# Turning the inverse softmax sums of the two larger tiles with a 32x32 block transpose, so that the context's factor is read in order

## The reference, cut to what matters

```python
scores = einsum('blhe,bmhe->bhlm', Q, K) / sqrt(E)
attn = softmax(scores + mask)                       # exp(..) / sum over the keys
ctx = einsum('bhlm,bmhe->blhe', attn, V)            # one context vector per token and head
y = gelu(ctx @ Wo + bo)
```

## Time and profile before

| | us |
|---|---|
| median of 3 runs | 646.54 (646.0 to 646.78) |
| the profiled execution, its own time | 644.08 |
| its span from the first to the last instruction | 642.3 |
| TensorE busy in the span | 604.5 (94%) |
| VectorE / ScalarE / GpSimd busy | 476.5 (74%) / 428.2 (67%) / 304.3 (47%) |
| share of the 16 DMA engines' time on queue q1 | 63.2% |

### The profile page before, as it was taken

One profiled execution on the slowest core, in us unless ns is written; L12 is line 12 of the kernel. 1 busy time (PEld: TensorE's weight loads), 2 busy tenths in 40 slices (PEclk: granted clock), 3 DMA queues, 4 the chain that ended last, 5 costly groups with the idle time before them and its releaser, 6 DMA issues.

```text
span 642.3 us, 10478 instructions
## 1 busy us (share of the span) xinstructions
PE 604.5 (94%) x3342; PEld 522.5 (81%) x3342; DVE 476.5 (74%) x1088; ACT 428.2 (67%) x1023; POOL 304.3 (47%) x244
## 2 busy tenths in 40 slices
PE   7799999999799999999999999999999999999661
PEld 5688888888679889888988888898888889898550
DVE  6545556543888778878998788899878889987546
ACT  4333444534788687677978777798877869887440
POOL 1000000000155654554689655468965547897454
PEclk9999999999899999999999999999999999999896
DMA  8330121020497789886678888857798895879840
GB/s 257 117 130 33 66 98 65 1 73 20 143 231 221 192 229 254 219 225 173 172 197 249 258 228 207 232 154 208 241 265 222 208 246 140 222 229 262 215 115 33
DMA packets 72501, 113.28 MB, mean 176 GB/s; under 512 B 11136, under 2 KB 50176, under 8 KB 70400
## 3 DMA queue, kind: packets, MB, share of 16 engines
q1 hardware_dynamic: 72016, 112.30, 63.2%
q10 hardware_dynamic: 432, 0.33, 0.2%
HBM read 66.40 MB, written 46.20 MB: 175 GB/s over the span
## 4 chain that ended last, share of the span: by engine, by line
PE 73%; DMA 13%; DVE 5%; POOL 3%; ACT 3%; SPq 2%; issue 1%; ACTq 0%; POOLq 0%
PE bank L1012 28%; PE down_ps L1012 13%; PE down_ps L1162 10%; DMA p_scratch<-probs 7%; PE down_ps L1072 7%; PE bank L1041 6%; PE bank L1039 6%; DMA probs<-p_scratch 4%; POOL pT_lo L565 3%; DMA raw<-in_wgu 2%; DVE probs L945 2%; PE bank L1123 2%; SPq L481 1%; ACT pT_hi L709 1%; DVE wgu_lo L802 1%
## 5 line engine op out<-in xcount | busy, mean ns | idle before, releaser
L565 POOL TENSOR_TENSOR pT_lo<-probs,pT_hi 128x512 fp32r<-128x512 f32 x160 | 204.3, 1297 | 86.9 <-ACT pT_hi L709 86.4
L699 ACT ACTIVATE probs<-probs,least 128x512 f32<-128x512 f32 (+3 forms) x256 | 141.0, 553 | 35.9 <-DVE least L930 35.6
L930 DVE CUSTOM_DVE_ANT_0 probs<-bank,mask 128x512 f32<-128x512 f32 (+3 forms) x256 | 116.0, 484 | 25.6 <-PE bank L1012 23.5
L577 POOL TENSOR_TENSOR probs<-probs,inv 128x1024 f32<-128x1024 f32 (+1 forms) x32 | 47.0, 1468 | 142.5 <-DVE inv L938 142.4
L709 ACT ACTIVATE pT_hi<-probs 128x512 fp32r<-128x512 f32 x160 | 95.9, 625 | 23.0 <-DMA probs<-p_scratch 17.5
L945 DVE STREAM_TRANSPOSE probs<-probs 128x2048 f32<-128x2048 f32 (+1 forms) x64 | 95.5, 1493 | 0.3 <-POOL probs L577 0.3
L1162 PE MATMUL down_ps<-wo_lo,cT_hi 128*128 128x256 f32 x256 | 73.9, 289 | 6.1 <-DVE cT_lo L970 6.0
L1162 PE MATMUL down_ps<-wo_hi,cT_hi 128*128 128x256 f32 x256 | 72.4, 283 | 0.0
L1162 PE MATMUL down_ps<-wo_hi,cT_lo 128*128 128x256 f32 x256 | 72.3, 283 | 0.0
L1012 PE MATMUL down_ps<-pT_lo,v_hi 128*128 128x512 f32 x160 | 65.9, 412 | 5.6 <-POOL pT_lo L565 5.4
L1012 PE MATMUL bank<-kT_lo,qT_hi 128*128 128x384 f32 (+1 forms) x192 | 66.0, 344 | 3.8 <-DVE least L930 3.3
(11 more groups left out here) (143 smaller groups left out, 1376.4 us busy)
## 6 DMA issues: line engine op xcount, KB each, us to landing
p_scratch<-probs SPq DMA_DIRECT2D x16, 1024.0 KB, 4.4
probs<-p_scratch SPq DMA_DIRECT2D x64, 256.0 KB, 4.9
p_scratch<-probs SPq DMA_DIRECT2D x16, 768.0 KB, 6.7
probs<-p_scratch SPq DMA_DIRECT2D x64, 192.0 KB, 4.0
inv_b<-i_scratch SPq DMA_DIRECT2D x32, 256.0 KB, 5.1
p_scratch<-probs SPq DMA_DIRECT2D x16, 512.0 KB, 3.1
probs<-p_scratch SPq DMA_DIRECT2D x64, 128.0 KB, 4.6
p_scratch<-probs SPq DMA_DIRECT2D x16, 256.0 KB, 4.7
```

Source lines behind the costliest of these rows:

```text
L565: nc.gpsimd.tensor_tensor(lo[:].rearrange("p (a n) -> p a n", a=BLOCKS), turned(t, j), f32(hi[:]).rearrange("p (a n) -> p a n", a=BLOCKS), ...
L577: nc.gpsimd.tensor_tensor(p, p, factor, ALU.mult).then_inc(probs_made, 1)
L699: nc.scalar.activation(p, p, ACT.Exp, bias=least[:, u, g:g + 1], scale=-1.0, accum_out=total[:, n * T + t, g:g + 1]).then_inc(exp_done, 1)
L930: nc.vector.tensor_tensor_reduce(out=head_of(t, g), in0=ps[:, 0:(t + 1) * P].rearrange("p (k i) -> p k i", i=BLOCK), in1=mask_of(t), scale ...
```

## The change

The inverses of tiles 2 and 3 go into the first 4 columns of a 128x32 tile that was set to zero once, VectorE turns this tile in 32x32 blocks, so that rows 0 to 3 of each block of 32 partitions hold one head's inverses of 32 tokens, and SyncE writes those four rows of each of the four blocks with a transfer of its own (4 rows of 128 B). The scratch in DRAM then lies in the order of the context bank, and so does `inv_b`.

```diff
+INV_ROWS = ranks([s for s in DVE_STEPS if s[0] == "ri" and s[2] not in NORMED], "ri")
...
+    inv_cols = [sb(f"inv_cols{i}", [P, BLOCK]) for i in range(2)]
+    inv_rows = [sb(f"inv_rows{i}", [P, BLOCK]) for i in range(2)]
...
-    inv_b = [sb(f"inv_b{i}", [P, P, G]) for i in range(INV_BUFFERS)]
+    inv_b = [sb(f"inv_b{i}", [P, BLOCKS, G, BLOCK]) for i in range(INV_BUFFERS)]
...
             elif kind == "IW":
                 t = step[2]
-                sp.wait_ge(inv_made, INVERTED["ri", n, t])
-                sp.dma_start(i_scratch[n % 2, t], inv[:, n % KV * T + t, :]).then_inc(inv_out[t], 16)
+                sp.wait_ge(inv_turned, INV_ROWS["ri", n, t])
+                for a in range(BLOCKS):
+                    sp.dma_start(i_scratch[n % 2, t, a], inv_rows[t - T // 2][a * BLOCK:a * BLOCK + G, :]).then_inc(inv_out[t], 16)
             elif kind == "IR":
                 t = step[2]
-                sp.wait_ge(inv_out[t], 16 * n + 16)
+                sp.wait_ge(inv_out[t], BLOCKS * 16 * (n + 1))
...
-                    nc.vector.reciprocal(inv[:, n % KV * T + t, :], total[:, n * T + t, :]).then_inc(inv_made, 1)
+                    if t in NORMED:
+                        nc.vector.reciprocal(inv[:, n % KV * T + t, :], total[:, n * T + t, :]).then_inc(inv_made, 1)
+                    else:
+                        i = t - T // 2
+                        nc.vector.reciprocal(inv_cols[i][:, 0:G], total[:, n * T + t, :]).then_inc(inv_made, 1)
+                        dve.wait_ge(inv_made, INVERTED["ri", n, t])
+                        if n:
+                            dve.wait_ge(inv_out[t], BLOCKS * 16 * n)
+                        nc.vector.transpose(inv_rows[i][:], inv_cols[i][:]).then_inc(inv_turned, 1)
...
-                    nc.vector.tensor_tensor(bank, bank, inv_b[INV_USE["c", n, t] % INV_BUFFERS][:].rearrange("p (a i) g -> p a g i", a=BLOCKS),
+                    nc.vector.tensor_tensor(bank, bank, inv_b[INV_USE["c", n, t] % INV_BUFFERS][:],
...
+        for cols in inv_cols:
+            nc.vector.memset(cols[:], 0.0)
         steps(DVE_STEPS)
...
-    i_scratch = nc.dram_tensor("i_scratch", (2, T, P, G), F32, kind="Internal").ap()
+    i_scratch = nc.dram_tensor("i_scratch", (2, T, BLOCKS, G, BLOCK), F32, kind="Internal").ap()
```

More of the change, by code:

```diff
@@ L318, in build @@
     inv_in = [sem(f"inv_in{t}") for t in range(T)]
+    inv_ready, inv_turned = sem("inv_ready"), sem("inv_turned")
     probs_made, turned_here, split_here = sem("probs_made"), sem("turned_here"), sem("split_here")
@@ L492, in _ @@
                     sp.wait_ge(ctx_scaled, use - INV_BUFFERS)
-                sp.dma_start(inv_b[use % INV_BUFFERS][:].rearrange("p q g -> p (q g)"),
-                             i_scratch[n % 2, t:t + 1].rearrange("u q g -> u (q g)").to_broadcast([P, P * G])
+                sp.dma_start(inv_b[use % INV_BUFFERS][:].rearrange("p a g i -> p (a g i)"),
+                             i_scratch[n % 2, t:t + 1].rearrange("u a g i -> u (a g i)").to_broadcast([P, P * G])
                              ).then_inc(inv_in[t], 16)
```

## The result

The changed kernel takes **641.84 us** (median of 4 executions, 639.54 to 642.36) against 646.66 us (4 executions, 646.0 to 647.54): a ratio of 0.9914, 95% interval 0.9885 to 0.9943. Forecast were 646.8 us and a range from 644.0 to 648.6.

The account below looks back on a forecast made before the run. TensorE was taken as the bound. +0.24 (first period) + 0.6 (later passages) - 0.6 (fewer packets) + 0 + 0 = +0.24 us, added to the median of three runs, gave 646.8 us; range 644.0 to 648.6.

Parts of the forecast that it names:

- Bound and place: Attention: TensorE is the bound, all waiting in the steady part is worth 4.4 us, the chain passes DRAM with tile 2.
- the sign of being wrong: Attention's 14 intervals: the prediction is wrong if together they change by more than 1 us from 395.4.
- Part 1: Context's multiplication on VectorE, factor read in order: 12.8 us less busy, worth nothing on the path.
- The sign that I named: VectorE ahead of the reciprocals: idle time goes up by several us, where the multiplication's gain goes.
- Part 2: Added transposes on VectorE: about 212 ns each, 6.8 us busy; what follows the reciprocal comes 0.24 us later.
- the 0.12 for each other passage: Chain's five later passages over DRAM: half of the 0.24 us delay counted for each, 0.6 us in all.
- Part 3: Inverse writes, four for one: 0 for SyncE; fewer packets save 0.1 us for each of six passages, -0.6.
- Rival A: Tile 2's DRAM passage shortens as 16 B packets stop occupying the queue: 642.4 at full 0.72 us, 644.6 at half; chance 0.24.
- Rival B: The 0.24 us behind tile 3's reciprocal passes on in full every period, 1.7 us: 648.4 us; chance 0.22.
- Rival C: The context's multiplication stays near 1097 ns, read order not being what it pays for: 647.1 us; chance 0.04.
- a later IR3: Read of tile 3's inverses, at 2.0 us per transfer: waits until about 1.5 us behind W3's issue, sum unchanged.

Follow-up runs that it names:

- w_only: The changed kernel, but the context's multiplication reads its factor with a step of four floats again: 640.79 us, ratio 0.9903 to the kernel before.
- c_only: The kernel before, but the context's multiplication reads its factor in order, with the old 128 writes of 16 B and no added transpose: 645.58 us, ratio 0.9983.
- w_tile3: The changed kernel, but only tile 3's inverses are turned and written in four pieces, tile 2's as before the change: 648.49 us, ratio 1.0027.
- iw2_late: The kernel before, but SyncE issues the write of tile 2's inverses behind the reads of tile 2's probabilities: 641.67 us, ratio 0.9933.
- the pitch kernels: The kernel before, inverse writes as 128 rows of 16 B at distances of 16, 32 or 64 B, broadcast read from the identity matrix: ratios 0.9980, 0.9922, 0.9903.
- wide_128B: The kernel before, but each write of the inverses is 128 rows of 128 B from the identity matrix: 639.96 us, ratio 0.9910.
- pitch_64B: The kernel before, inverse writes as 128 rows of 16 B lying 64 B apart, broadcast read from the identity matrix: 640.93 us, ratio 0.9903.
- few_16: The kernel before, but each write of the inverses is one transfer of 16 rows of 128 B from the identity matrix: 639.50 us, ratio 0.9902.

## Why the prediction was wrong

**Bound and place: right.** TensorE was named as the bound, the 4.4 us in the steady part as all there was to win there, and the passage of tile 2 over DRAM as the chain's way. That is where it was won. But the sign of being wrong came: the 14 intervals together were not to change by more than 1 us, and they lost 1.4 (from 192.91 to 588.51 before, from 191.56 to 585.72 after).

**Part 1: right.** 12.8 us less on VectorE in "c" were forecast and measured (35.1 to 22.3), with little or nothing on the path. `w_only` has the gain without it, `c_only` is at 0.9983. That the step of four floats is what costs the 401 ns, worked out from two rows then, is shown by these two kernels, which differ from after and before in nothing but the step of "c": 1098 ns with it and 698 without. The sum for the engine was off: "6 us less busy" was forecast, the page has 475.8 against 476.5. The groups that the change touches do give 6.0 (-12.8, +6.8); the instructions that make `xn_b` (L847 before, L852 now) went from 9.1 to 12.0 us, and the rest I haven't followed up. The sign that I named, longer idle time ahead of the reciprocals, didn't come: 24.4, now 8.4 + 12.6 = 21.0.

**Part 2: right in size.** 212 ns and 0.24 us were forecast, 212 ns and 0.25 measured. In the first period they lie on the path in full: from the 12 matmuls at 157.61 us to "tt3" at 165.81 were 8.20 us before, and from 156.50 to 164.94 they are 8.44. Whether the 0.12 for each other passage is right was not isolated; the loss of `w_tile3` allows it and doesn't show it.

**Part 3: this is the step that failed.** The prediction held the 128 writes against the queue only by the time that they occupy it, "at most 0.72 us, at least for nearly nothing", took 0.1 for each passage, and argued that "IW2 is over by then". The premise was that what stands behind a transfer can't hold up its landing. `iw2_late`, `w_tile3` and the pitch kernels show that it does: W2 lands 1.0 us later in the median, 0.8 us in the mean from W2 to R2, if 128 rows of 16 B side by side are written right behind it. IW2 wasn't over by then either: its landing follows W2's by some 0.2 us in each period before. The term should have been about -0.8 for each passage, limited by what each period has to give, in place of -0.1; with six passages that is at most 4.8 us, and the profiled pair gained 3.4 in the attention and at the end. I had taken a mean packet, 0.09 us; the records of the single packets show 9 ns for one of 16 B (4096 of them in the trace before), so occupation was worth 0.07 us per write, less than even the 0.1. The price was in the addresses.

**Rival A: right in outcome, not in its reason.** It had the shorter passage, 644.6 us at half price and 642.4 in full, with a chance of 0.24; measured are 641.84. Its mechanism, the engines' time taken by the packets, is refuted by `wide_128B`, with as many packets, and by `pitch_64B`. That its full price, 0.72 us a passage, is close to the 0.8 measured is luck: it was made of the mean packet's 0.09 us, and a packet of 16 B takes a tenth of that. The range stopped a little below its half price, although the full price was written down; it should have reached there. **Rival B** wasn't shown: the loss of `w_tile3` would fit it, but no run had the later "ri3" alone. Its 1.7 us also counts six passages beside the first period where part 2 has five; it should read 1.4. **Rival C** was wrong, "c" became faster as it should.

The Trainium skill's advice against many small transfers (DMA: Bandwidth & Descriptors, Rules for kernel authors) didn't decide: four transfers of 512 B were no worse than the one of `few_16` within the intervals, and SyncE issued them in 1.26 us where nothing stood ahead, hidden behind "tt3" as forecast. The Trainium skill's fixed 2.0 us (DMA: Bandwidth & Descriptors, Anatomy of one DMA, where it is given for transfers issued from GpSimd), from which the prediction estimated a later IR3, wasn't seen: IR3 started 0.44 us behind W3 in the median, before and after, and 1.7 us behind the start of the last piece for which it waits.

**What stays open.** The runs show where the time goes, between the end of W2's last packet and its landing, but not why: whether the engines wait for each other, or DRAM serves neighbouring 16 B writes slowly and the end of W2 with them. Rows side by side were tried at 16, 64, 128 and 512 B, so nothing between 16 and 64, and rows of 16 B at distances of 16, 32, 64 and 512 B. A larger distance also spreads the 128 rows over a longer stretch of DRAM (2 KB, 4 KB, 8 KB, 64 KB); the two weren't taken apart, except that 16 rows of 128 B in 2 KB cost nothing (`few_16`).

## What to carry to other kernels

A tiny transfer isn't priced by its bytes or by the time that it occupies the queue. If many rows of 16 B are written side by side in DRAM (128 here), the transfer ahead of them can land up to a microsecond later, so give such rows a pitch of 64 B (32 B did most of it here), write them as fewer and wider rows, or issue them where nobody waits for the landing ahead. When a chain over DRAM sets the time, take apart what is issued just behind the transfer that is waited for, and not only what is ahead.

## What the runs showed of the hardware that wasn't expected

- 128 writes of 16 B side by side in DRAM, issued 0.55 us behind a write of 768 KB, put its landing off to 6.3 to 7.2 us in the median; with the same rows 32, 64 or 512 B apart, with rows of 64, 128 and 512 B side by side, or with the writes elsewhere in the queue it is 5.5 to 6.0.
- The delay sits behind the data: from the end of the last packet to the landing it is 1.20 to 1.42 us with such neighbours, 0.48 to 0.51 without and 0.67 at a distance of 32 B.
- Going below 512 B a row had no price in time that could be measured here down to 64 B, nor at 16 B with a distance.
- A packet of 16 B occupies an engine for 9 ns and one of 128 B for 12, where the mean packet of this kernel takes 90.
- VectorE reads a float32 operand with a step of four floats at 1097 ns for 128x512, in order at 698, beside a PSUM operand and result.
